# Attention stage: the transposes of a batch's probabilities all one period later, queries and keys last in a period

## The chip, the cores and the metric

The kernel runs on one core of one Trainium2 chip. The metric is the device time of one execution in microseconds. TensorE (PE in the rows, PEld its weight loads), VectorE (DVE), ScalarE (ACT), GpSimd (POOL) and SyncE (SP, which issues DMAs) each run their own queue in order and wait for one another by semaphores.

## The reference

The program is one transformer-like block on 64 images with text tokens: a tokenizer (patches, local and global attention) gives 5 tokens of 256 channels per image, 77 text tokens are joined to them, so T = 82 tokens per batch entry and 64 entries; then attention with a relative bias, then a mixture of 8 low-rank experts. The change is in the attention:

```python
qkv = (xn @ w_qkv + b_qkv).reshape(b, t, 3, H, hd)        # b 64, t 82, H 16 heads of hd 16
q, k, v = (qkv[0], qkv[1], qkv[2])
scores = jnp.einsum('bhqd,bhkd->bhqk', q, k) * scale
attn = jax.nn.softmax(scores + bias, axis=-1)             # bias: a function of query - key, per head
out = jnp.einsum('bhqk,bhkd->bhqd', attn, v)
out = jnp.transpose(out, (0, 2, 1, 3)).reshape(b, t, dim)
return out @ w_out + b_out
```

xn is a layer norm of a layer norm of the tokens; the result is added to the tokens. All in f32.

## The kernel before

Three blocks follow one another, with a barrier between: tokenizer (to about 205 us), attention (to about 667 us), experts. `attention_block` holds the 64 x 82 = 5248 tokens as 41 tiles of 128 and works in periods, one per batch entry b, with three more to drain (`for b in range(NB + 3)`). The order within a period is written out by hand, separately for each engine; an engine does its work in that order and waits where a semaphore isn't there yet.

The pieces of TensorE's work, all in f32, are:
- `xT(n)` transposes a normalised token tile n (one tile in 41 of the periods); ScalarE copies it to `hT` (`copy_xT`). GpSimd normalises the tile (`prepare`) and VectorE makes its statistics (`normal_stats`).
- `qk(q, j)` makes the queries (j = 0, 1) or keys (j = 2, 3) of half of the heads, for four batch entries at once (a quad q, 328 tokens): four products a quad, one per period, in the quad before. VectorE reads each with two instructions that scale it and add bias terms (`read_qk`, L981) into `qT` or `kT`, which hold two quads.
- `val(b)` makes the values of one entry; ScalarE copies them to `vv` (`copy_val`).
- `scores(b)` makes the 16 score matrices of 82 x 82 in four banks `psS` (32 small matmuls, L825). It waits for the last read of its quad's queries and keys, and for the reads of the scores of b - 1.
- VectorE's `shift(b, half)` takes the largest score of each row and subtracts it, in two halves, into `prob`; ScalarE's `exponent(b, half)` takes the exponential in place.
- `turn(b, g)`, g = 0 to 3, transposes four of the 16 matrices into `psP` (L834), which is one bank; ScalarE copies it to `probT` (`copy_probT`, L934), and the next turn waits for that copy.
- `weigh(b)` multiplies `probT` by the values (L847) and by ones (L852), which gives outputs and denominators, each denominator repeated over the 32 channels of its head pair. VectorE's `normalise` takes the reciprocal (L1005) and multiplies.
- `project(n)` is the output projection of a token tile (in 41 of the periods, three behind); ScalarE copies it and GpSimd adds it to the tokens.

`xT`, `qk`, `val` and `project` share two banks `psQ` in turn: `uses` lists them in TensorE's order, a use takes bank `place % 2` and waits in `free` until the use before the last has been read, by ScalarE or, for `qk`, by VectorE. `turned(b)` and `projected(b)` give the tiles of a period.

TensorE's order in period b: scores(b), weigh(b - 2), turn(b - 1, 2), xT, qk, turn(b - 1, 3), val(b + 1), turn(b, 0), project, turn(b, 1). The last two turns of an entry are so made one period after its first two. There is no qk from period 60 on. ScalarE's order matches: copy turn 2, copy tile, exponent 0, copy turn 3, exponent 1, copy values, copy turn 0, copy projection, copy turn 1. VectorE's: shift 0, shift 1, read qk, normalise(b - 2), statistics.

Of the kernel before, what the change touches and what calls it, by code (L numbers as in the profile page):

```python
# [13 lines left out]
NB, CIN, IMG = 64, 3, 96  # L14
# [622 lines left out]
def attention_block(nc, S, I, A, W, H, ident_all, out):  # L637

    NTL = NB * T // 128
    NQ = NB // 4  # L640
# [6 lines left out]
    def turned(b):  # L647
        return [n for n in range(NTL) if turn_at[n] == b]

    def projected(b):  # L650
        return [n for n in range(NTL) if last_of[n] == b - 3]
# [7 lines left out]
    uses = [("xT", 0), ("xT", 1), ("xT", 2)] + [("qk", j) for j in range(4)] + [("val", 0), ("xT", 3), ("xT", 4), ("xT", 5)]  # L659
    for b in range(NB + 3):  # L660
        uses += [("xT", n) for n in turned(b)]
        if b // 4 + 1 < NQ:
            uses.append(("qk", 4 * (b // 4 + 1) + b % 4))
        if b + 1 < NB:
            uses.append(("val", b + 1))
        uses += [("project", n) for n in projected(b)]
    place = {use: k for k, use in enumerate(uses)}
    by_act = {use: 1 + sum(u[0] != "qk" for u in uses[:k]) for k, use in enumerate(uses) if use[0] != "qk"}
    by_dve = {use: 1 + sum(u[0] == "qk" for u in uses[:k]) for k, use in enumerate(uses) if use[0] == "qk"}

    with ExitStack() as ctx:
# [30 lines left out]
        def bank(use):  # L702
            return psQ[:, place[use] % 2, :]
# [67 lines left out]
        def _(te):  # L771
# [16 lines left out]
            def xT(n):  # L788

                te.wait_ge(S["xh_ready"], n + 1)  # L790
                free(("xT", n))
                for c in range(2):
                    mm = te.transpose(bank(("xT", n))[:, 128 * c:128 * c + 128], xh[:, n % 3, 128 * c:128 * c + 128], ident_all[:])
                mm.then_inc(S["xT_done"], 1)
# [11 lines left out]
            def val(b):  # L806

                te.wait_ge(S["psQ_act"], by_act["xT", tiles_of[b // 4]])
                free(("val", b))
                a = T * b % RH  # L810
                for c in range(2):
                    mm = te.matmul(bank(("val", b))[0:T, 0:C], hT[:, c, a:a + T], wv[:, c, :], start=(c == 0), stop=(c == 1))  # L812
                mm.then_inc(S["val_done"], 1)
# [15 lines left out]
            def turn(b, g):  # L829

                te.wait_ge(S["prob_ready"], 2 * b + g // 2 + 1)
                te.wait_ge(S["probT_ready"], 4 * b + g)
                for s in range(4):
                    mm = te.transpose(psP[0:T, s * T:s * T + T], prob[:, b % 2, g, s, :], ident_all[0:T, 0:T])  # L834
                mm.then_inc(S["turn_done"], 1)
# [20 lines left out]
            def project(n):  # L856

                te.wait_ge(S["att_ready"], last_of[n] + 1)
                free(("project", n))
                a = 128 * n % RA  # L860
                for c in range(2):
                    mm = te.matmul(bank(("project", n))[:, 0:C], attT[:, c, a:a + 128], wout[:, c, :], start=(c == 0), stop=(c == 1))  # L862
                mm.then_inc(S["project_done"], 1)
# [8 lines left out]
            for b in range(NB + 3):  # L872
                if b < NB:
                    scores(b)
                if 0 <= b - 2 < NB:
                    weigh(b - 2)
                if 0 <= b - 1 < NB:
                    turn(b - 1, 2)
                for n in turned(b):
                    xT(n)  # L880
                if b // 4 + 1 < NQ:
                    qk(b // 4 + 1, b % 4)
                if 0 <= b - 1 < NB:
                    turn(b - 1, 3)
                if b + 1 < NB:
                    val(b + 1)
                if b < NB:
                    turn(b, 0)
                for n in projected(b):
                    project(n)  # L890
                if b < NB:
                    turn(b, 1)

        @block.scalar
        def _(act):
            def copy_xT(n):

                act.wait_ge(S["xT_done"], n + 1)
                done = (128 * n + 128 - RH + T - 1) // T
                if done > 0:  # L900
                    act.wait_ge(S["val_done"], done)
                for a, lo, size in pieces(128 * n, 128, RH):
                    ins = act.activation(hT[:, :, a:a + size],  # L903
                                         bank(("xT", n))[:, 0:256].rearrange("p (c t) -> p c t", c=2)[:, :, lo:lo + size], ACT.Copy)
                ins.then_inc(S["psQ_act"], 1)

            def copy_val(b):

                act.wait_ge(S["val_done"], b + 1)
                if b >= 4:  # L910
                    act.wait_ge(S["weigh_done"], b - 3)
                v4 = bank(("val", b))[0:T, 0:C].rearrange("p (s a d) -> p s a d", s=8, a=2)
                pair = vv[:, b % 4, :, :, :].rearrange("p s a (h d) -> p s (a h) d", h=2)[:, :, 0:4:3, :]
                act.activation(pair, v4, ACT.Copy).then_inc(S["psQ_act"], 1)

            def copy_project(n):

                act.wait_ge(S["project_done"], n + 1)
                if n >= 2:
                    act.wait_ge(S["res_ready"], n - 1)  # L920
                act.activation(po[:, n % 2, :], bank(("project", n))[:, 0:C], ACT.Copy).then_inc(S["psQ_act"], 1)  # L921

            def exponent(b, half):

                act.wait_ge(S["shifted"], 2 * b + half + 1)
                act.activation(prob[:, b % 2, 2 * half:2 * half + 2, :, :], prob[:, b % 2, 2 * half:2 * half + 2, :, :],  # L926
                               ACT.Exp).then_inc(S["prob_ready"], 1)

            def copy_probT(b, g):

                act.wait_ge(S["turn_done"], 4 * b + g + 1)
                if g == 0 and b >= 2:
                    act.wait_ge(S["weigh_done"], b - 1)
                act.activation(probT[:, b % 2, g, :, :].rearrange("p s t -> p (s t)"), psP[0:T, 0:4 * T],  # L934
                               ACT.Copy).then_inc(S["probT_ready"], 1)

            for n in range(3):
                copy_xT(n)
            act.wait_ge(S["vv_clear"], 1)
            copy_val(0)  # L940
            for n in range(3, 6):
                copy_xT(n)
            for b in range(NB + 3):
                if 0 <= b - 1 < NB:
                    copy_probT(b - 1, 2)
                for n in turned(b):
                    copy_xT(n)
                if b < NB:
                    exponent(b, 0)
                if 0 <= b - 1 < NB:  # L950
                    copy_probT(b - 1, 3)
                if b < NB:
                    exponent(b, 1)
                if b + 1 < NB:
                    copy_val(b + 1)
                if b < NB:
                    copy_probT(b, 0)
                for n in projected(b):
                    copy_project(n)
                if b < NB:  # L960
                    copy_probT(b, 1)

        @block.vector
        def _(v):
# [9 lines left out]
            def read_qk(q, j):  # L974

                v.wait_ge(S["qk_done"], 4 * q + j + 1)
                if q >= 2:
                    v.wait_ge(S["scores_done"], 4 * (q - 1))
                dst, scal, add, t = (qT, ownq, qadd, j) if j < 2 else (kT, own, kadd, j - 2)
                for a in range(2):  # L980
                    ins = v.scalar_tensor_tensor(out=dst[:, q % 2, a, t, :].rearrange("p (b t) -> p b t", b=4),  # L981
                                                 in0=bank(("qk", 4 * q + j))[:, 0:QT].rearrange("p (b t) -> p b t", b=4),
                                                 scalar=scal[:, a:a + 1], in1=add[:, a, t, :].unsqueeze(1).to_broadcast([128, 4, T]),
                                                 op0=ALU.mult, op1=ALU.add)
                ins.then_inc(S["psQ_dve"], 1)
# [55 lines left out]
            for b in range(NB + 3):  # L1041
                if b < NB:
                    shift(b, 0)
                    shift(b, 1)
                if b // 4 + 1 < NQ:
                    read_qk(b // 4 + 1, b % 4)
                if 0 <= b - 2 < NB:
                    normalise(b - 2)
                for n in turned(b + 2):
                    if n not in early:  # L1050
                        normal_stats(n)


def expert_block(nc, S, I, R, W, H, ident_all, out):
# [439 lines left out]
```

## Time and profile before

| | us |
|---|---|
| median of 3 runs | 861.71 |
| lowest, highest | 855.84, 864.61 |
| the profiled execution | 861.1 |
| its span, first to last instruction | 859.3 |

The page of a profile gives each engine's busy time first, then the span in slices. The order of time lists instructions by their start; neighbours of one line are merged (x32 is 32 instructions), their time runs from the first's start to the last's end, and what stands in brackets is how long the engine was idle before them and what ended that. Matmuls overlap their neighbours by some tenths of a microsecond, so what a piece of work costs TensorE is read from start to start. Windows give busy time by stretch, with the granted TensorE clock, 1.00 being full speed.

### The profile page before, as it was taken

What the parts mean: (1) busy time and instruction counts of PE and PEld (TensorE: products, weight loads), DVE (VectorE), ACT (ScalarE), POOL (GpSimd) and SP (SyncE); (2) the same over time, 40 slices, a digit from 0 to 9 for tenths busy, and PEclk for the clock granted to TensorE, in tenths of its full rate; (3) what the DMA queues carried; (4) which work ended last, traced back from release to release, by engine and by line L of the source; (5) the groups of instructions that cost most, each with busy time, mean ns of one, the idle gap of its engine ahead of it and who ended that gap; (6) DMA issues with size and microseconds to landing.
All of it is one profiled execution on the core that took longest, in us unless ns stands there. A gap on an engine that the chain in (4) does not pass through costs nothing. (4 is left out here: it accounts for less than half of the span.)

```text
span 859.3 us, 24631 instructions
## 1 busy us (share of the span) xinstructions
PE 690.2 (80%) x10030; PEld 527.5 (61%) x10030; DVE 599.7 (70%) x1199; ACT 349.9 (41%) x793; POOL 285.6 (33%) x361
## 2 busy tenths in 40 slices
PE   1769696461479999999999999999988479999960
PEld 1657543320257777777777777777766368888850
DVE  0627657843459899999899998998885246766525
ACT  1211111000035555555555555555454335555533
POOL 2474200002272333333233333332000455667333
PEclk9879899675779999999999999999998769999995
DMA  8990100005910000000000000000000412222117
GB/s 158 225 311 8 37 1 0 1 12 178 306 23 8 15 16 14 15 16 21 14 9 21 15 15 16 15 15 15 21 14 15 98 56 74 71 81 76 51 65 272
DMA packets 34786, 51.42 MB, mean 60 GB/s; under 512 B 9044, under 2 KB 26292, under 8 KB 34548
## 3 DMA queue, kind: packets, MB, share of 16 engines
q1 hardware_dynamic: 29524, 39.57, 16.2%
q0 software_dynamic: 5152, 10.29, 4.2%
q8 instruction: 81, 1.33, 0.6%
q14 instruction: 29, 0.24, 0.1%
HBM read 36.91 MB, written 18.00 MB: 64 GB/s over the span
## 5 line engine op out<-in xcount | busy, mean ns | idle before, releaser
L934 ACT ACTIVATE probT<-psP 82x328 f32<-82x328 f32 x256 | 112.1, 438 | 161.4 <-PE psP L834 161.4
L993 DVE TENSOR_REDUCE mx<-psS 82x8 f32<-82x656 f32 x128 | 106.5, 832 | 42.4 <-PE psS L825 42.2
L834 PE MATMUL psP<-ident_all,prob 82*82 82x82 f32 x1024 | 117.3, 236 | 22.5 <-ACT probT L934 22.4
L834 PEld LDWEIGHTS psP<-ident_all,prob 82*82 82x82 f32 x1024 | 89.8, 120 | 65.6 <-issue 25.9
L755 POOL TENSOR_TENSOR h_flat<-h_flat,po 128x256 f32<-128x256 f32 x41 | 29.7, 725 | 263.7 <-ACT po L921 263.7
L995 DVE TENSOR_TENSOR prob<-psS,mx 82x656 f32<-82x656 f32 x128 | 107.1, 837 | 4.4
L926 ACT ACTIVATE prob<-prob 82x656 f32<-82x656 f32 x128 | 94.8, 741 | 3.1 <-DVE prob L995 3.1
L802 PE MATMUL psQ<-hT,early 128*128 128x328 f32 x256 | 83.1, 449 | 0.6 <-ACT hT L903 0.5
L1005 DVE RECIPROCAL rden<-psO 128x164 f32<-128x164 f32 x64 | 74.8, 1169 | 4.4 <-PE psO L852 4.4
L812 PE MATMUL psQ<-early,hT 128*82 128x256 f32 x256 | 66.7, 383 | 0.1
L825 PE MATMUL psS<-kT,qT 32*82 32x82 f32 x2048 | 53.6, 242 | 0.0
L802 PEld LDWEIGHTS psQ<-hT,early 128*128 128x128 f32 x256 | 44.2, 192 | 13.1 <-issue 1.3
L742 POOL TENSOR_SCALAR xh<-h_flat,a_mv,a_rst 128x256 f32<-128x256 f32 x41 | 50.2, 1224 | 4.5
L847 PE MATMUL psO<-probT,vv 82*32 82x82 f32 x2048 | 50.7, 239 | 0.5 <-ACT probT L934 0.5
L1269 ACT ACTIVATE f_hT<-psH 128x1024 f32<-128x1024 f32 x39 | 39.9, 1024 | 26.4 <-PE psH L1198 26.4
L862 PE MATMUL psQ<-wout,attT 128*128 128x256 f32 x164 | 46.7, 410 | 4.1 <-DVE kT L981 1.9
L1131 POOL DMA_INDIRECT entry_rows<-yv,slot_entry x39 | 39.9, 1023 | 30.2 <-ACT yv L1276 24.1
L852 PE MATMUL psO<-probT,one 82*32 82x82 f32 x2048 | 49.0, 236 | 0.0
L825 PEld LDWEIGHTS psS<-kT,qT 32*82 32x82 f32 x2048 | 43.8, 149 | 7.4 <-issue 0.3
L1210 PE MATMUL psT<-f_hT,w2as 128*64 128x128 f32 x624 | 44.5, 286 | 3.6 <-DVE t L1351 3.6
L1198 PE MATMUL psH<-t1T,w1bs 64*128 64x128 f32 x624 | 46.8, 291 | 0.0
L227 PE MATMUL tk_ps<-early 128*128 128x256 f32 (+1 forms) x180 | 45.9, 407 | 0.0
(218 smaller groups left out, 1216.5 us busy)
## 6 DMA issues: line engine op xcount, KB each, us to landing
img<-in_x SPq DMA_DIRECT2D x6, 1008.0 KB, 19.5
out<-h_flat SPq DMA_DIRECT2D x41, 128.0 KB, 2.5
fused_rows<-in_txt SPq DMA_DIRECT2D x1, 4928.0 KB, 25.1
h_flat<-entry_rows SPq DMA_DIRECT2D x6, 512.0 KB, 6.5
h_flat<-fused_rows SPq DMA_DIRECT2D x1, 2176.0 KB, 16.2
ex_w2a<-in_ff_w_A SPq DMA_DIRECT2D x1, 2048.0 KB, 11.2
ex_w1b<-in_ff_w_B SPq DMA_DIRECT2D x2, 1024.0 KB, 16.7
out<-h_flat SPq DMA_DIRECT2D x8, 256.0 KB, 4.8
```

Source lines behind the costliest of these rows:

```text
L742: pool.tensor_scalar(xh[:, n % 3, :], H[:, n, :], mv[:, n % 4, 0:1], rst[:, n % 4:n % 4 + 1], ALU.subtract, ALU.mult).then_inc(S["xh_ready ...
L802: mm = te.matmul(bank(("qk", 4 * q + j))[:, 0:QT], wqkv[:, c, 128 * j:128 * j + 128], hT[:, c, a:a + QT], start=(c == 0), stop=(c == 1))
L812: mm = te.matmul(bank(("val", b))[0:T, 0:C], hT[:, c, a:a + T], wv[:, c, :], start=(c == 0), stop=(c == 1))
L825: mm = te.matmul(psS[0:T, g, s:s + T], qT[rows, par, a, t, cols], kT[rows, par, a, t, cols], start=True, stop=True)
L834: mm = te.transpose(psP[0:T, s * T:s * T + T], prob[:, b % 2, g, s, :], ident_all[0:T, 0:T])
L847: te.matmul(psO[32 * g:32 * g + 32, t * T:t * T + T], vv[:, b % 4, 4 * t + g, a, :], probT[:, b % 2, g, 2 * t + a, :], start=(a == 0), sto ...
L852: mm = te.matmul(psO[32 * g:32 * g + 32, (2 + t) * T:(3 + t) * T], one2[:, a, :], probT[:, b % 2, g, 2 * t + a, :], start=(a == 0), stop=( ...
L926: act.activation(prob[:, b % 2, 2 * half:2 * half + 2, :, :], prob[:, b % 2, 2 * half:2 * half + 2, :, :], ACT.Exp).then_inc(S["prob_ready ...
L934: act.activation(probT[:, b % 2, g, :, :].rearrange("p s t -> p (s t)"), psP[0:T, 0:4 * T], ACT.Copy).then_inc(S["probT_ready"], 1)
L993: v.tensor_reduce(mx[:, half, :, :], s4, X, ALU.max).then_inc(S["max_ready"], 1)
L995: v.tensor_tensor(prob[:, b % 2, 2 * half:2 * half + 2, :, :], s4, mx[:, half, :, :].unsqueeze(3).to_broadcast([T, 2, 4, T]), ALU.subtract ...
L1005: v.reciprocal(rden[:], o3[:, 1, :, :]).then_inc(S["rden_ready"], 1)
```

## The change

In TensorE's order all four turns of entry b - 1 are made in period b, in the order scores(b), weigh(b - 2), turn 0, xT, val(b + 1), turn 1, project, turn 2, qk, turn 3. `uses` is rearranged so that qk is the last use of a period. ScalarE's order becomes copy turn 0, copy tile, copy values, copy turn 1, exponent 0, copy projection, copy turn 2, exponent 1, copy turn 3. VectorE reads qk last in a period, behind `normalise` and the statistics. No instruction is added or taken away; how denominators are made (spread over channels by `one2`) stays. The diff:

```diff
--- before.py
+++ after.py
@@ -659,11 +659,11 @@
     uses = [("xT", 0), ("xT", 1), ("xT", 2)] + [("qk", j) for j in range(4)] + [("val", 0), ("xT", 3), ("xT", 4), ("xT", 5)]
     for b in range(NB + 3):
         uses += [("xT", n) for n in turned(b)]
-        if b // 4 + 1 < NQ:
-            uses.append(("qk", 4 * (b // 4 + 1) + b % 4))
         if b + 1 < NB:
             uses.append(("val", b + 1))
         uses += [("project", n) for n in projected(b)]
+        if b // 4 + 1 < NQ:
+            uses.append(("qk", 4 * (b // 4 + 1) + b % 4))
     place = {use: k for k, use in enumerate(uses)}
     by_act = {use: 1 + sum(u[0] != "qk" for u in uses[:k]) for k, use in enumerate(uses) if use[0] != "qk"}
     by_dve = {use: 1 + sum(u[0] == "qk" for u in uses[:k]) for k, use in enumerate(uses) if use[0] == "qk"}
@@ -875,21 +875,21 @@
                 if 0 <= b - 2 < NB:
                     weigh(b - 2)
                 if 0 <= b - 1 < NB:
-                    turn(b - 1, 2)
+                    turn(b - 1, 0)
                 for n in turned(b):
                     xT(n)
+                if b + 1 < NB:
+                    val(b + 1)
+                if 0 <= b - 1 < NB:
+                    turn(b - 1, 1)
+                for n in projected(b):
+                    project(n)
+                if 0 <= b - 1 < NB:
+                    turn(b - 1, 2)
                 if b // 4 + 1 < NQ:
                     qk(b // 4 + 1, b % 4)
                 if 0 <= b - 1 < NB:
                     turn(b - 1, 3)
-                if b + 1 < NB:
-                    val(b + 1)
-                if b < NB:
-                    turn(b, 0)
-                for n in projected(b):
-                    project(n)
-                if b < NB:
-                    turn(b, 1)
 
         @block.scalar
         def _(act):
@@ -942,23 +942,23 @@
                 copy_xT(n)
             for b in range(NB + 3):
                 if 0 <= b - 1 < NB:
-                    copy_probT(b - 1, 2)
+                    copy_probT(b - 1, 0)
                 for n in turned(b):
                     copy_xT(n)
+                if b + 1 < NB:
+                    copy_val(b + 1)
+                if 0 <= b - 1 < NB:
+                    copy_probT(b - 1, 1)
                 if b < NB:
                     exponent(b, 0)
+                for n in projected(b):
+                    copy_project(n)
+                if 0 <= b - 1 < NB:
+                    copy_probT(b - 1, 2)
+                if b < NB:
+                    exponent(b, 1)
                 if 0 <= b - 1 < NB:
                     copy_probT(b - 1, 3)
-                if b < NB:
-                    exponent(b, 1)
-                if b + 1 < NB:
-                    copy_val(b + 1)
-                if b < NB:
-                    copy_probT(b, 0)
-                for n in projected(b):
-                    copy_project(n)
-                if b < NB:
-                    copy_probT(b, 1)
 
         @block.vector
         def _(v):
@@ -1042,13 +1042,13 @@
                 if b < NB:
                     shift(b, 0)
                     shift(b, 1)
-                if b // 4 + 1 < NQ:
-                    read_qk(b // 4 + 1, b % 4)
                 if 0 <= b - 2 < NB:
                     normalise(b - 2)
                 for n in turned(b + 2):
                     if n not in early:
                         normal_stats(n)
+                if b // 4 + 1 < NQ:
+                    read_qk(b // 4 + 1, b % 4)
 
 
 def expert_block(nc, S, I, R, W, H, ident_all, out):
```

## Rows read from the trace of the kernel before

**Rows 1.** The page, part 1: busy us, share of the span, instructions.
```profile
PE 690.2 (80%) x10030; PEld 527.5 (61%) x10030; DVE 599.7 (70%) x1199; ACT 349.9 (41%) x793; POOL 285.6 (33%) x361
```

**Rows 2.** Windows: stretch, length, busy us (instructions) by engine, granted clock, DMA.
```profile
300.00:600.00 300.00, 285.58 (x5696) 226.28 (x5695) 272.80 (x432) 163.35 (x384) 96.65 (x141) 1.00 0.05 16
...
659.00:662.00 3.00, 2.04 (x52) 1.89 (x56) 1.03 (x3) 0.72 (x2) 0.00 (x0) 0.70 0.10 32
```

**Rows 3.** Order of time, period 25: start, us, engine, line, operation, idle before.
```profile
404.59 0.83 PE L825 MATMUL psS<-kT,qT 32*82 32x82 f32 x32
...
405.35 0.78 PE L847 MATMUL psO<-probT,vv 82*32 82x82 f32 x32
...
405.49 0.84 DVE L993 TENSOR_REDUCE mx<-psS 82x8 f32<-82x656 f32 x1 [0.36 <-PE psS L825]
...
406.63 0.48 PE L834 MATMUL psP<-ident_all,prob 82*82 82x82 f32 x4
...
406.95 0.38 PE L793 MATMUL psQ<-ident_all,xh 128*128 128x128 f32 x2
...
407.18 1.27 PE L802 MATMUL psQ<-hT,early 128*128 128x328 f32 x4
...
408.28 0.45 PE L834 MATMUL psP<-ident_all,prob 82*82 82x82 f32 x4
...
408.56 1.03 PE L812 MATMUL psQ<-early,hT 128*82 128x256 f32 x4
...
408.73 1.01 DVE L981 SCALAR_TENSOR_TENSOR qT<-psQ,ownq,qadd 128x328 f32<-128x328 f32 x2
...
409.11 0.74 ACT L926 ACTIVATE prob<-prob 82x656 f32<-82x656 f32 x1
...
409.43 0.45 PE L834 MATMUL psP<-ident_all,prob 82*82 82x82 f32 x4
...
410.01 0.44 ACT L934 ACTIVATE probT<-psP 82x328 f32<-82x328 f32 x1
...
410.59 0.46 PE L834 MATMUL psP<-ident_all,prob 82*82 82x82 f32 x4 [0.71 <-ACT probT L934]
...
410.98 0.83 PE L825 MATMUL psS<-kT,qT 32*82 32x82 f32 x32
```

**Rows 4.** Order of time, period 27, which has a projection and no tile.
```profile
417.60 0.83 PE L825 MATMUL psS<-kT,qT 32*82 32x82 f32 x32
...
419.96 1.31 PE L802 MATMUL psQ<-hT,early 128*128 128x328 f32 x4
...
421.11 0.45 PE L834 MATMUL psP<-ident_all,prob 82*82 82x82 f32 x4
...
421.74 1.01 DVE L981 SCALAR_TENSOR_TENSOR kT<-psQ,own,kadd 128x328 f32<-128x328 f32 x2
...
422.26 0.45 PE L834 MATMUL psP<-ident_all,prob 82*82 82x82 f32 x4
...
422.90 1.10 PE L862 MATMUL psQ<-wout,attT 128*128 128x256 f32 x4 [0.19 <-DVE kT L981]
...
423.84 0.45 PE L834 MATMUL psP<-ident_all,prob 82*82 82x82 f32 x4
...
424.22 0.83 PE L825 MATMUL psS<-kT,qT 32*82 32x82 f32 x32
```

**Rows 5.** Order of time at the stage's start and in its last periods.
```profile
248.60 1.22 POOL L742 TENSOR_SCALAR xh<-h_flat,a_mv,a_rst 128x256 f32<-128x256 f32 x1
...
654.32 0.45 PE L834 MATMUL psP<-ident_all,prob 82*82 82x82 f32 x4 [0.62 <-ACT probT L934]
...
654.81 0.44 ACT L934 ACTIVATE probT<-psP 82x328 f32<-82x328 f32 x1
...
660.41 1.32 PE L847 MATMUL psO<-probT,vv 82*32 82x82 f32 x32 [0.53 <-ACT probT L934]
```

## The prediction

> **What bounds the kernel now.** I read the page first, then the engines' busy time by windows, then the order of time through single periods of the attention stage. The page gives TensorE 80% of the span, the most of any engine [rows 1]. The change touches the attention stage alone, which holds 64 periods between 241 and 660 us, so the windows matter more: between 300 and 600 us TensorE is busy 285.58 of 300 us at a granted clock of 1.00 (full speed, 2.4 GHz), VectorE 272.80 and ScalarE 163.35 [rows 2]. TensorE's order sets the pace, and VectorE has some 9% to spare. The order of time through one period shows how. I count from the start of `scores`: for a period with a token tile and no projection [rows 3] the starts are scores 0, weigh 0.76, turn 2.04, token tile 2.36, qk 2.59, turn 3.69, val 3.97, turn 4.84, turn 6.00, and the next scores 6.39. So what follows what costs, start to start: scores 0.76, weigh 1.28, turn 0.32 before a token tile, token tile 0.23, qk 1.10 (1.15 where it follows a turn directly [rows 4]), turn 0.28 before val, val 0.87, turn 0.38 before scores, projection 0.94 [rows 4]. The exception is a turn that follows a turn with nothing between: 4.84 to 6.00, of which the row puts 0.71 down to the wait for ScalarE's copy, since `psP` is one bank and the copy must empty it. With a projection between the two turns that wait goes, but the projection starts 0.64 after its turn, 0.19 of it waiting for VectorE's read of the qk bank [rows 4].
>
> By `turned` and `projected`, periods 2 to 59 are 17 with a token tile only (6.39 us each), 16 with tile and projection (410.98 to 417.60: 6.62), 20 with a projection only (417.60 to 424.22: 6.62) and 5 with neither (6.39 less the tile: 6.2) [rows 3, 4].
>
> **The new order on TensorE, steady periods.** Nothing is added or removed: the same matmuls, copies and reads, no DMA moved. The order becomes scores, weigh, T0, tile, val, T1, projection, T2, qk, T3. All four turns work on exponentials of the period before, so none waits for an exponential any more; T0 to T1 is covered by val, T2 to T3 by qk, T1 to T2 by the projection only, where there is one.
>
> A bare turn pair costs 1.10: where ScalarE is free the copy starts 0.49 after the turn, and the next turn starts 0.58 after that copy does [rows 3, 5], 1.07; 1.16 was seen behind another copy; I take 1.10. Then:
> - Projection only: T0 2.04, val 2.36, T1 3.23, projection 3.55, T2 4.49, qk 4.81, T3 5.96, scores 6.34. Before 6.62: 0.28 less, times 20 is 5.6.
> - Tile and projection: the tile adds 0.23, so 6.57: 0.05 less, times 16 is 0.8.
> - Tile only: T1 3.46, T2 4.56 (bare pair), qk 4.88, T3 6.03, scores 6.41: 0.03 more, times 17 is 0.5.
> - Neither: T1 3.23, T2 4.33, scores 6.18: 0.02 less, times 5 is 0.1.
> Sum: 6.0 us less. The gain is small, since the wait for the copy moves from the last pair of turns to T1 and T2 and stays 0.7 long in 22 periods; what goes is the projection's wait for the qk bank. Bounds: with 1.07 to 1.16 for the bare pair the 22 periods give -0.7 to +1.3, and every start being read to 0.01 or 0.02 gives another 1, so 4 to 8 less.
>
> Does ScalarE keep up? In its new order (copy T0, copy tile, copy val, copy T1, exponential 0, copy projection, copy T2, exponential 1, copy T3) the longest chain is: val ends about 3.6, its copy to 4.0, copy T1 about 3.97 to 4.4, exponential 0 from 4.3 (its input is there since about 2.6, half-way through the shifts, which end by 4.14 [rows 3]), copy T2 at 5.05 to 5.25, exponential 1 about 5.4 to 6.2, copy T3 at T3 + 0.49. Each copy is there when TensorE wants it. The tightest is new: weigh of the next period needs copy T3, ready 1.07 to 1.10 after T3 starts, and weigh comes 0.38 + 0.76 = 1.14 after T3. That is a tie with 0.04 to spare. I cost it at nothing; if the cover is short by 0.05 it costs 3 us over 58 periods.
>
> **The wait that is added.** The queries and keys of the next four batches are made one product per period, the fourth in periods 3, 7, ... 59. `scores` of the period after reads them at once: it waits for `by_dve["qk", 4*(b//4)+3]`. Before, that read began at 4.14 and ended at 5.15 [rows 3], long before scores at 6.4. Now qk starts last but one, at 4.8 to 5.05; its matmuls take 1.31 [rows 4]; a VectorE instruction starts about 0.07 after the last matmul it waits for (scores 0 + 0.83, reduction 0.90 [rows 3]); the two reads last 1.01; and TensorE goes on 0.15 after the end of such a read (421.74 + 1.01 to 422.90 [rows 4]). That is 2.54 from the start of qk to scores, against 1.15 + 0.38 = 1.53 by TensorE's own order. So 1.01 us of pause in each of 15 periods: 15.2 us more. VectorE is free to read at once: its 272.80 us over some 46 periods [rows 2] are 5.93 a period, 1.01 of it these reads; the other 4.9, begun at 0.90, end near 5.9, before qk's matmuls do (6.1 to 6.4). Behind the waiting scores stand weigh and all four turns of the period, and VectorE and ScalarE, which live on them; nothing catches up, because the other periods are TensorE's own order. In the other periods the read hides: it ends where the scores are just done (qk + 2.4 against 1.53 + 0.90 = 2.43). Bounds: 0.85 if the matmuls' modelled end is late by 0.15, 1.2 if statistics come in the way: 13 to 18 us.
>
> **Ends of the stage.** At the start the two turns of period 0 leave it, and scores of period 1 no longer wait for exponentials. But the token tile of period 1 comes from GpSimd, whose normalisation runs 248.60 to 249.82 whatever TensorE does [rows 5], and it now stands ahead of val and all but one turn. So of 2.5 us by TensorE's order I keep 0.9 less (bounds 0 to 2.5). At the end period 64 has four turns, bare, where it had two: 2 x 1.10 = 2.2 more, and 0.7 for the weigh ahead of them, whose last turn was bare too. Against it stand 0.65 less over periods 60 to 63 (0.16, 0.33 and 0.16, the fourth is in the 0.7). The last weigh already ran at 0.70 of the clock, 1.32 instead of 0.78 us for one half [rows 2, 3, 5]; with two more turns at low load I add 0.5. Sum of the end: 2.75 more (2 to 4).
>
> **On the clock.** In [rows 2] it stayed at 1.00 through 300 us with a pause of 0.71 in most of the periods without a projection, and was down in the last 3 us of the stage, where two bare turns and a wait stood in a row. The Trainium skill ("TensorE: Matmul & The Clock Gate", part 4, PE-mode transpose) says that transposes don't count as a busy engine for the clock; by that, four of them in a row are worse than two, and the trace agrees in kind with its 0.70. The 0.5 us above comes from the rows alone; by the rule it would be nearer to 1.5.
>
> **Sum.** -6.0 + 15.2 - 0.9 + 2.75 = +11.0 us. The profiled execution took 861.1 us, the median of the runs shown is 861.71, so the two can be taken as one: 861.7 + 11.0 = 872.7, which I give as 872.5.
>
> **The rivals.**
> - A. The mechanism as summed, 872.5. For it: the wait is in the code, all its parts have rows. Own range 866 to 879. Chance 0.72.
> - B (the other side). The pause before scores is hidden: the fourth qk read ends in time and costs nothing. Then -6.0 - 0.9 + 2.75 = -4.2, 857.5, faster than before though within 1%. It decides the sign where the pause is under 0.28 us. It would need the read to start before qk's matmuls end. Against it: qk is last but one and one turn of 0.38 is all its cover. Chance 0.07.
> - C. Weigh waits for the copy of T3 in every period, because the exponential 1 ahead of that copy on ScalarE is late. The exponential lasts 0.74 [rows 3] and has about 0.4 to spare; were it used up and the copy 0.25 late, 58 x 0.25 = 14.5 more: 887. For it: the tie of 0.04. Chance 0.12.
> - D. The turns gain more than I see: the bare pair T1 and T2 costs no more than a covered one (22 x 0.75 = 16.5 less than summed): 856. Against it: `psP` stays one bank and the bare pair has a row at 0.62 of wait even where ScalarE is idle [rows 5]. Chance 0.04.
> - E. The 1 us pauses drop the clock. One half of weigh takes 1.32 instead of 0.78 at the lower level (1.2 GHz) [rows 3, 5], a factor of 1.7; a period of 6.4 would become about 10.8, and 15 of them add 66: 938. The Trainium skill ("TensorE: Matmul & The Clock Gate", HAM oscillation) ties a fall to gaps longer than these. Against it: pauses of 0.71 left the clock at 1.00 [rows 2, 3]. Chance 0.03. 0.02 remain for what I have not thought of.
>
> **How the numbers follow.** The likeliest is A, 872.5. The range 865 to 881 takes A's bounds (13 - 8 - 2.5 + 2 = +4.5 to 18 - 4 + 0 + 4 = +18, rarely all at one end) and the mild part of C; it leaves out B, D, E and the rest of C, about 2 in 10. About 1% (8.6 us: under 853.1, over 870.3) is what a measurement of this kernel can tell from no change. Slower by over 1%: seven in ten of A, 0.50, and C, E, 0.14: 0.64. Faster by over 1%: half of D and a little of B, 0.03. Within: 0.33.
>
> **What would show it.** Right: scores starts in the periods after 3, 7, ... wait about 1.0 us for VectorE's `kT` read (L981), some 15 us in the table of waits; projection's wait for `qT`/`kT` gone; TensorE's wait for the copies of `probT` stays near 18 us; periods with projection only 6.3 us, tile only 6.4; TensorE busy share between 300 and 600 us falls a little. Wrong: scores not waiting at all (B), `psO` matmuls waiting for `probT` (C), turns of 0.3 us spacing in periods without projection (D), a granted clock under 1.00 between 300 and 600 us (E).

## The result, and the profile after

| | before | after |
|---|---|---|
| median, us | 859.22 (9 runs) | 866.81 (9 runs) |
| lowest, highest | 855.84, 864.61 | 863.58, 868.17 |
| the profiled execution | 861.1 | 866.31 |
| its span | 859.3 | 864.5 |

The ratio is 1.008, with a 95% interval of 1.0055 to 1.0105: the change costs 0.8%, some 7 us. The prediction was 872.5 us (865 to 881), so slower it is, by less than forecast: within 1%, to which it gave a chance of 0.33, and not over 1%, to which it gave 0.64.

The wait that the prediction put at every fourth period is there. This is who waited for whom in the kernel after between 240 and 640 us (engine and line, what it waited for: us in total, times, longest):

```profile
PEld psS L825 <- DVE kT L981: 15.4, 15, 1.1
PE psP L834 <- ACT probT L934: 14.3, 23, 0.6
PE psS L825 <- DVE kT L981: 12.7, 15, 0.9
```

`scores` waits 15 times for the `kT` read, 12.7 us together (0.83 to 0.91 each); the wait of a turn for its copy is still there (23 times, up to 0.6, where [rows 3] had 0.71); the projection's wait for the qk bank [rows 4] is in no line any more. The same in order of time, in the kernel after, from the last turns of period 3 (which ends a quad) through period 4 (projection, no tile) to the next scores:

```profile
265.47 0.45 PE L834 MATMUL psP<-ident_all,prob 82*82 82x82 f32 x4 [0.62 <-ACT probT L934]
265.76 1.31 PE L802 MATMUL psQ<-hT,early 128*128 128x328 f32 x4
...
266.90 0.45 PE L834 MATMUL psP<-ident_all,prob 82*82 82x82 f32 x4
...
267.10 1.02 DVE L981 SCALAR_TENSOR_TENSOR kT<-psQ,own,kadd 128x328 f32<-128x328 f32 x2
...
268.18 0.83 PE L825 MATMUL psS<-kT,qT 32*82 32x82 f32 x32 [0.83 <-DVE kT L981]
...
269.08 0.83 DVE L993 TENSOR_REDUCE mx<-psS 82x8 f32<-82x656 f32 x1 [0.95 <-PE psS L825]
...
271.42 0.45 PE L834 MATMUL psP<-ident_all,prob 82*82 82x82 f32 x4
...
271.70 1.07 PE L862 MATMUL psQ<-wout,attT 128*128 128x256 f32 x4
...
272.61 0.45 PE L834 MATMUL psP<-ident_all,prob 82*82 82x82 f32 x4
...
272.89 1.31 PE L802 MATMUL psQ<-hT,early 128*128 128x328 f32 x4
...
274.04 0.45 PE L834 MATMUL psP<-ident_all,prob 82*82 82x82 f32 x4
...
274.42 0.83 PE L825 MATMUL psS<-kT,qT 32*82 32x82 f32 x32
```

qk starts at 265.76, its read at 267.10, 1.34 later; the read ends at 268.12 and scores starts at 268.18. VectorE then waits 0.95 itself for those scores. The next period has none of this: the projection follows its turn by 0.28 (0.64 in [rows 4]) and the whole period takes 6.24 us instead of 6.62. Over the steady stretch the two effects nearly cancel: 300 us hold 5692 matmuls, where they held 5696. The window of the kernel after (columns as in [rows 2]):

```profile
300.00:600.00 300.00, 280.77 (x5692) 225.60 (x5691) 274.38 (x431) 164.46 (x383) 96.66 (x141) 1.00 0.05 16
```

Read from start to start of scores, the periods 2 to 59 of both kernels, mean us of each kind:

| kind | before | after | after, where the next quad begins |
|---|---|---|---|
| projection only (20) | 6.62 | 6.23 | 7.18 (5 of them) |
| tile and projection (16) | 6.62 | 6.45 | 7.35 (4) |
| tile only (17) | 6.39 | 6.33 | 7.24 (5) |
| neither (5) | 6.2 | 6.1 to 6.25 | 7.01 (1) |

And the attention stage in four parts, from traces of one execution each (starts of scores of periods 0, 2, 60, 63, and of the last projections):

| kernel | 0 to 2 | 2 to 60 | 60 to 63 | 63 to the last projections | sum |
|---|---|---|---|---|---|
| before | 13.58 | 377.97 | 18.41 | 11.58 | 421.54 |
| after | 15.46 | 379.91 | 19.22 | 14.58 | 429.17 |

The stage is 7.6 us longer, as much as the medians differ (7.6). The two spans differ by 5.2 only, because the profiled execution of the kernel after began its attention work 1.7 us sooner (its first matmul at 221.24 instead of 222.98, after DMAs that the change doesn't touch).

### The profile page after: what moved, and what is told of

It reads as the page before. It is cut to its first block and busy times, and to the rows that moved or that the text cites. A ratio compares the mean times of both kernels' runs of the same rounds, so it can differ in the third digit from the quotient of the medians.

```text
span 864.5 us, 24631 instructions
## 1 busy us (share of the span) xinstructions
PE 689.2 (80%) x10030; PEld 530.6 (61%) x10030; DVE 603.6 (70%) x1199; ACT 352.1 (41%) x793; POOL 286.4 (33%) x361
## 5 line engine op out<-in xcount | busy, mean ns | idle before, releaser
L802 PE MATMUL psQ<-hT,early 128*128 128x328 f32 x256 | 85.4, 458 | 0.6 <-ACT hT L903 0.5
L825 PE MATMUL psS<-kT,qT 32*82 32x82 f32 x2048 | 53.8, 242 | 12.7 <-DVE kT L981 12.7
```

The costliest lines, as they stand in the source:

```text
L802: mm = te.matmul(bank(("qk", 4 * q + j))[:, 0:QT], wqkv[:, c, 128 * j:128 * j + 128], hT[:, c, a:a + QT], start=(c == 0), stop=(c == 1))
L825: mm = te.matmul(psS[0:T, g, s:s + T], qT[rows, par, a, t, cols], kT[rows, par, a, t, cols], start=True, stop=True)
```

## The experiments

Theory Q is that of the prediction: the cost is scores waiting for the fourth qk read, and the gain is the projection no longer waiting for the qk bank; both come from qk standing last, none from the turns. Its rival R: the gain comes from the turns, which no longer depend on exponentials of their own period. Each ratio is to runs of the kernel before in the same series. In one series the kernel before took 907.0 us, some 45 us longer, outside the attention stage: with the tile first, it has there 377.86 us between scores 2 and 60 and 421.39 in the four parts together (421.54 in the table). The four kernels of that series (the fourth product alone last, the tile first in the kernel before, the last turns, the three together) are read by their ratio and by the parts of the stage only.

**One part alone: the turns.**

```diff
-                    turn(b - 1, 2)
+                    turn(b - 1, 0)
...
-                    turn(b - 1, 3)
+                    turn(b - 1, 1)
...
-                if b < NB:
-                    turn(b, 0)
+                if 0 <= b - 1 < NB:
+                    turn(b - 1, 2)
                 for n in projected(b):
                     project(n)
-                if b < NB:
-                    turn(b, 1)
+                if 0 <= b - 1 < NB:
+                    turn(b - 1, 3)
```

This is against the kernel before, whose `uses` and VectorE order it keeps; ScalarE's copies of the turns follow.

> One part alone: all four turns in the period after, but qk and its read where the kernel before has them (behind the token tile; VectorE reads ahead of normalise); order scores, weigh, turn 0, tile, qk, turn 1, val, turn 2, projection, turn 3. Theory Q (the cost is scores waiting for the fourth qk read, the gain is the projection no longer waiting for the qk bank): both are gone here, since the projection again follows qk by one use and scores waits for nothing. Periods with a projection 6.6 us, with a tile only 6.3, no wait of scores, and the costs of the stage's ends (3 to 5 us) stay: 0 to +4 us against before. Rival R (what gains is that turns no longer depend on the exponentials of their own period): periods with a projection fall to 6.2 to 6.45 here too, and the time is 5 to 10 us under before.

Measured 864.8 us, ratio 1.003 (1.0005 to 1.0055). Between scores 2 and 60 it takes 377.94 us, the kernel before 377.97; periods with a projection are 6.62, with a tile only 6.39. Who waited, between 300 and 600 us:

```profile
PE psP L834 <- ACT probT L934: 12.1, 17, 0.7
PE psQ L862 <- DVE kT L981: 1.4, 7, 0.2
```

The projection waits for the qk bank as before and scores waits for nothing. The last part is 15.19 us instead of 11.58. So the turns a period later bring nothing in the steady periods and cost some 3 us at the end: rival R falls.

**The other part alone: qk last.**

```diff
-                    turn(b - 1, 0)
+                    turn(b - 1, 2)
...
-                    turn(b - 1, 1)
+                    turn(b - 1, 3)
...
-                if 0 <= b - 1 < NB:
-                    turn(b - 1, 2)
+                if b < NB:
+                    turn(b, 0)
                 if b // 4 + 1 < NQ:
                     qk(b // 4 + 1, b % 4)
-                if 0 <= b - 1 < NB:
-                    turn(b - 1, 3)
+                if b < NB:
+                    turn(b, 1)
```

This is against the changed kernel, whose `uses` and VectorE order it keeps; ScalarE's copies of the turns follow, and exponential 0 goes ahead of the copy of the values.

> The other part alone: turns 0 and 1 of an entry stay in its own period, qk and its read go to the end; ScalarE takes exponential 0 ahead of the copy of the values, so that turn 0 has it in time. Order scores, weigh, turn 2, tile, val, turn 3, projection, turn 0, qk, turn 1. Theory Q: 15 waits of scores of 0.9 us as in the changed kernel, periods 6.2 to 6.45 otherwise, as the changed kernel; the tail is as before, so 3 to 4 us under the changed kernel: +2 to +5 against before. Rival R: without the turns a period later the steady periods stay at 6.4 to 6.6, and with the 15 waits the time is +12 to +16 against before.

Measured 869.34 us, ratio 1.0102 (1.0062 to 1.0142), some 8 us over before: more than the 2 to 5 that Q gave, less than the 12 to 16 of R. The waits between 240 and 640 us:

```profile
PEld psS L825 <- DVE kT L981: 15.4, 15, 1.1
PE psS L825 <- DVE kT L981: 12.7, 15, 0.9
```

The 15 waits are those of the changed kernel to the tenth, and a period with a projection only is 6.23 again, though the turns stand where they stood before. The last part is 11.62, as before. Two things make it slower than expected: periods with a tile are 6.48 instead of 6.33 and 6.45 (383.28 us between scores 2 and 60, 3.4 more than the changed kernel), since my order for ScalarE puts an exponential ahead of the values' copy; and the granted clock of this execution fell to 0.50 in period 62 (9.07 us instead of 6.13). The steady part speaks for Q: the gain of 0.39 in projection-only periods and the 12.7 us of wait both belong to qk alone.

**The wait alone, in the kernel before.**

```diff
-                if b // 4 + 1 < NQ:
+                if b // 4 + 1 < NQ and b % 4 < 3:
                     qk(b // 4 + 1, b % 4)
...
                 for n in projected(b):
                     project(n)
+                if b // 4 + 1 < NQ and b % 4 == 3:
+                    qk(b // 4 + 1, b % 4)
                 if b < NB:
                     turn(b, 1)
```

> The kernel before with the wait alone: in periods 3, 7, ... 59 the fourth qk product goes between the projection and turn 1, and its read to the end of VectorE's period; the other 49 periods and the turns stay as they were. Theory Q: scores waits 0.8 to 0.9 us of TensorE's own time 15 times for the kT read; those periods are 0.6 to 0.9 us longer (the projection's wait for the qk bank goes in the nine that have one), +9 to +13 against before. Rival (the pause is made up in the next periods): under +4.

Ratio 1.0165 (1.0118 to 1.0212), 14 us. Of the waits, the part between 300 and 600 us:

```profile
PE psP L836 <- ACT probT L938: 13.8, 23, 0.7
PE psS L827 <- DVE kT L985: 9.2, 11, 0.8
```

The stage is 393.98 us long between scores 2 and 60, 16.0 more than before: the 43 other periods are unchanged to 0.01 us and the 15 are 0.73 (tile only) to 1.34 us longer (7.12, 7.88, 7.96). Nothing is made up in the next period; that rival falls. It is more than I expected, because with qk gone from between turns 2 and 3 the second of them waits for the copy in these 15 periods, 0.62 us where nothing is left between the two and 0.40 where a tile is. So the edit adds more than the wait under test: between scores 2 and 60, `scores` waits 12.6 us for the read, and the turns wait 18.6 us in place of 15.6.

**The wait taken away from the changed kernel.** Each product one period earlier:

```diff
-                if b // 4 + 1 < NQ:
-                    qk(b // 4 + 1, b % 4)
+                if b + 5 < 4 * NQ:
+                    qk((b + 5) // 4, (b + 5) % 4)
```

`uses` and `read_qk` follow, and qk(1, 0) and its read stand ahead of period 0.

> The changed kernel with the one suspected wait taken away: each qk product is made one period earlier (product b + 5 instead of b + 4; the first of quad 1 ahead of period 0), so that the fourth of a quad is read a whole period before its scores. Same work. Theory Q: the 15 waits (12.7 us on TensorE in its row, 13.8 by period lengths) go, nothing else changes but 0 to 2 us at the start: 12 to 14 us under the changed kernel, some 6 under before. Rival: if the wait only moved work that VectorE must do anyway, the loop is then held by VectorE (busy 5.9 of 6.2 us a period) and under 6 us are gained.

Measured 853.07 us, ratio 0.9911 (0.9877 to 0.9944): against the changed kernel's 1.008 that is 1.7%, 14 us. Between scores 2 and 60 it takes 365.68 us, 14.2 less than the changed kernel, and the ends of quads are now as long as the other periods (6.23, 6.33, 6.45). 0.3 of the 14.2 is period 59 (5.93 us), which has no product any more. The price of the wait is read from this stretch; the medians hold more than the wait, since in the traces the start is 2.4 us shorter too, period 62 is 1.6 shorter at full clock and the end is 0.6 longer. The window and what is left of the waits:

```profile
300.00:600.00 300.00, 289.44 (x5893) 232.93 (x5895) 283.63 (x444) 170.66 (x396) 98.10 (x143) 1.00 0.05 16
```

```profile
PE psP L834 <- ACT probT L935: 10.6, 17, 0.6
```

VectorE goes from 274.38 to 283.63 of 300 us and still doesn't hold the loop, so that rival falls as well. Taking the wait away gives back 14 us, and adding it costs 12.6 us in its own row, inside a total of 14 to 16 us that holds other waits too: this step is settled.

**The start.** The stage's first two periods were 1.9 us longer after the change, where 0.9 less was forecast. TensorE in period 1 of the kernel after, and two windows:

```profile
247.90 0.44 PE L793 MATMUL psQ<-ident_all,xh 128*128 128x128 f32 x2 [1.54 <-POOL xh L742]
248.17 1.87 PE L812 MATMUL psQ<-early,hT 128*82 128x256 f32 x4
...
251.75 2.47 PE L802 MATMUL psQ<-hT,early 128*128 128x328 f32 x4
...
254.69 0.96 PE L825 MATMUL psS<-kT,qT 32*82 32x82 f32 x32
```

```profile
248.00:251.00 3.00, 2.59 (x10) 1.56 (x10) 1.96 (x4) 1.20 (x5) 1.47 (x3) 0.53 0.00 0
251.00:254.00 3.00, 2.79 (x8) 1.85 (x9) 0.00 (x0) 1.78 (x4) 1.95 (x2) 0.50 0.00 0
```

It waits 1.54 us for the tile from GpSimd and then the clock is at its lower level (0.50, 1.2 GHz) for six microseconds, val takes 1.87 and qk 2.47. Theory H: the wait for the tile made the clock fall. The test lets GpSimd prepare that tile first:

```diff
+            for n in turned(1):
+                prepare(n)
             for n in early:
                 add_row(n)
...
-                        prepare(n)
+                        if b > 0:
+                            prepare(n)
                         add_row(n)
```

> The changed kernel with one thing at the start: GpSimd normalises the token tile of period 1 before the seven additions of the bias row (4.8 us) instead of behind them. Theory H (the start lost 3 us against the prediction because TensorE waited 1.5 us for that tile and the granted clock then fell to 0.50 until 254 us): no wait of the tile, clock 1.00 from period 1 on, scores 0 to scores 2 about 12.5 instead of 15.5 us: 3 us under the changed kernel. Rival: the clock falls anyway, since the first periods are thin; then 0 to 1.5 us are gained.

```profile
248.49 0.39 PE L796 MATMUL psQ<-ident_all,xh 128*128 128x128 f32 x2
248.71 1.04 PE L815 MATMUL psQ<-early,hT 128*82 128x256 f32 x4
...
250.95 1.31 PE L805 MATMUL psQ<-hT,early 128*128 128x328 f32 x4
...
252.47 0.83 PE L828 MATMUL psS<-kT,qT 32*82 32x82 f32 x32
```

No wait, val 1.04, qk 1.31, and scores 0 to 2 take 11.15 instead of 15.46 us: 4.3 less, more than the 3 expected. The median is 861.63 us, ratio 1.001 (0.9987 to 1.0033), 0.7% under the changed kernel's; in the traces 1.6 us more are period 62, which was at the lower clock in the changed kernel's and isn't here. The control is the same edit in the kernel before:

> Control to the run with the tile first: the kernel before with the same change of GpSimd's order at the start. There TensorE waited 0.16 us for the tile of period 1 and its clock was at 1.00 by then. If the 3 to 5 us gained in the changed kernel came from the wait that the changed order made: 0 to 0.5 us gained here, within 1 us of before. Rival (the additions of the bias row slow VectorE or ScalarE in both kernels): 3 us gained here too.

Ratio 0.9991 (0.9964 to 1.0018), scores 0 to 2 in 13.54 instead of 13.58 us: nothing. So it is the changed order, which asks for the tile sooner, that ran into GpSimd; the turns alone a period later do it too (the tile waited for 1.51 us). That the wait of 1.5 us brings the clock down each time isn't shown. With the turns alone later it came down too (qk 2.29 us, scores 0 to 2 in 14.34). Of two kernels below with the changed kernel's order in period 1, the one with the denominators moved waited 1.48 us and took 15.33 us from scores 0 to 2 at the lower clock (qk 2.47); the one with the last turns moved waited 1.43 us and took 12.68, at full clock in period 1 (val to the next turn 0.86). So the clock fell behind three of the four such waits, and in no kernel whose wait there was under 1 us.

**The end.** The turns 0 and 1 of the last entry alone back in period 63, behind its turn 3 (period 64 leaves them out, and ScalarE's copies follow):

```diff
                 if 0 <= b - 1 < NB:
                     turn(b - 1, 3)
+                if b == NB - 1:
+                    turn(b, 0)
+                    turn(b, 1)
```

> The changed kernel with turns 0 and 1 of the last entry alone back in their own period (63), behind its turn 3, so that period 64 has two turns as before. If the longer end of the stage (3 us in period 63 and after) comes from the two bare turns that moved into period 64: the two turns are bare in period 63 just as well and stand ahead of the weigh that waits for the copy of turn 3, whose wait they now cover: 0.7 to 1.2 us less from scores 63 to the last projection, the other 2 us stay. Rival (it is the lower clock of thin periods): no gain, the distance from scores 63 to the last projection stays at 14.6 us, give or take 1.

No gain, where 0.7 to 1.2 us were expected: 14.56 us from scores 63 to the last projections, 14.58 in the changed kernel; ratio 1.0067 (1.0034 to 1.01). The total is the rival's number, but the parts are not. The wait of the first weigh is covered (weigh starts 0.38 us behind its turn instead of 0.98), and the 0.6 us so gained are lost behind it at the lower clock, where the second half of that weigh takes 1.02 us instead of 0.75 and the next two turns start 1.39 us apart instead of 1.10. This is how the stage ends in the kernel after:

```profile
663.72 0.45 PE L834 MATMUL psP<-ident_all,prob 82*82 82x82 f32 x4 [0.62 <-ACT probT L934]
664.79 0.74 PE L834 MATMUL psP<-ident_all,prob 82*82 82x82 f32 x4 [0.62 <-ACT probT L934]
666.06 1.32 PE L847 MATMUL psO<-probT,vv 82*32 82x82 f32 x32 [0.53 <-ACT probT L934]
```

A turn takes 0.45 us and 0.74 a microsecond later. The end holds eight turns from scores 63 on where the kernel before has six, and takes 3.0 us more: 2.1 for the two bare turns, 0.6 for the wait of the first weigh and 0.3 for the lower clock behind the last turn. In all traces it took 14.56 to 15.40 us with eight turns and 10.97 to 11.62 with six. That it makes no difference where the two stand isn't shown, since the clock differed.

**The three together**, qk one period ahead, GpSimd's tile first and the last turns moved (the diffs above):

> The changed kernel with all three: qk one period ahead, GpSimd's tile of period 1 first, turns 0 and 1 of the last entry in period 63. If the three costs are separate, 853.1 of the first alone less 0.5 to 1 for the end; the start was already without a pause there (tile wait gone since qk stood ahead of it), so nothing for the tile: 852, ratio to before 0.990.

Ratio 0.9929 (0.9901 to 0.9957), no better than the wait taken away alone (0.9911). The edits aren't separate: scores 0 started 23.2 us after the stage's first matmul, 18.0 in the changed kernel and 21.0 with qk one period ahead alone. That this comes from qk(1, 0) ahead of period 0 together with a tile more to prepare is likely, but no run parts the two.

**A version that beats both.** What remains of TensorE's waits is the bare pair. In the periods without a projection, the denominators' half of weigh (its second loop, now a function of its own) can stand between turns 1 and 2:

```diff
+            def denominators(b):
...
                 if 0 <= b - 2 < NB:
                     weigh(b - 2)
+                    if projected(b) or b >= NB:
+                        denominators(b - 2)
...
                     turn(b - 1, 1)
+                if 0 <= b - 2 < NB and not (projected(b) or b >= NB):
+                    denominators(b - 2)
```

> The changed kernel with the bare pair covered: in the 22 periods without a projection the second half of weigh (the denominators, 0.69 us) stands between turns 1 and 2, where TensorE waits 0.62 us for ScalarE's copy. If the bare pair costs what its row says, these periods fall from 6.33 to 5.65 by TensorE's order; VectorE (5.9 us of work a period) then holds some of it back: 6.33 to 5.9, 22 x 0.4 = 9 us under the changed kernel, at most 15. Rival (VectorE already sets the steady pace through the scores bank): under 3 us gained.

> qk one period ahead as in the run before it, but the first product of quad 1 inside period 0 instead of ahead of it (two products in period 0). Same steady periods as that run; the start of the stage 1 to 3 us shorter: ratio to before 0.988 (that run: 0.991).

> Both together: qk one period ahead and the bare pair covered by the denominators. TensorE's order asks for 5.65 us in periods without a projection and 6.23 to 6.45 in the others; VectorE asks for about 6.0 on average: a mean of 6.1 to 6.2 over 58 periods against 6.33 now, 8 to 12 us under the run before it: ratio to before 0.975 to 0.98. Rival: VectorE holds the loop at 6.3, then no gain.

The first, in the changed kernel: 854.78 us, ratio 0.9951 (0.9923 to 0.9979); periods with a tile only 5.81 instead of 6.33, with neither 5.59 instead of 6.12, 10.6 us less between scores 2 and 60. The expectations of the other two mean by "the run before it" the one with qk one period ahead, and for the third the second. The second has the first product of quad 1 inside period 0 (`products(0)` is [4, 5], then b + 5): 851.55 us, 0.9911 (0.9887 to 0.9934), the steady part 365.78 us, as there; the start was 2.7 us longer in scores 0 to 2 and 2.8 shorter ahead of it, so nothing came of moving it. The third, both: 837.96 us, ratio 0.9752 (0.9733 to 0.9771), 354.22 us between scores 2 and 60, 11.6 less than the second. The medians are 13.6 apart, over the 8 to 12 expected; in the traces period 62 is another 1.6 us shorter, at full clock. Its window:

```profile
300.00:600.00 300.00, 300.00 (x6072) 240.18 (x6065) 290.31 (x455) 175.60 (x406) 97.31 (x142) 1.00 0.05 17
```

TensorE waits for nothing in 300 us, and VectorE is at 290 of 300: in this stretch the order is at the end of what covering TensorE's waits can give. It is 2.5% under the kernel before and 3.3% under the changed one.

## Why the prediction was right, and where its sizes were off

**The wait.** Right in place and count, 15.2 us forecast. It is 13.8 by the lengths of periods (about 0.90 to 0.95 each), 13.9 by the run that takes it away, without its period 59. The step mis-sized is the handing on: 2.54 from the start of qk to scores, measured 2.42. TensorE went on 0.06 after the end of the read, not 0.15; the 0.15 of [rows 4] was not such a hand-over alone.

**The gain in the steady periods.** Forecast 6.0 us less, bounds 4 to 8; measured 11.9 (20 x 0.39, 16 x 0.17, 17 x 0.06, 5 x 0.08). The mechanism was right: the projection's wait goes and the bare pair stays at 0.62. The size came out beyond the bounds. It failed on hundredths: I took 0.32 for the step from a turn to what follows it, which [rows 3] show only for the turn behind weigh; behind the other turns it is 0.28 (there too, 408.28 to 408.56). The projection is 0.91 and not 0.94, the bare pair 1.07 and not 1.10. That makes 0.06 to 0.12 a period, and 58 periods make 5.9 us of it. My bound of 1 us for reading errors leaves room for 0.02 a period at most, and a step read from the wrong place stood several times in each.

**The start.** Forecast 0.9 less, measured 1.9 more. I saw that the tile came at 249.82 [rows 5] and took that only as a limit on the gain. The step that failed is that I gave this wait no price beyond the time it lasts: in the traced execution the clock was low for 6 us behind it. Where it stayed up behind the same wait (the last turns moved), scores 0 to 2 took 12.68 us, 0.9 less than before, as forecast; so nearly all of the 2.8 us is the clock's. Why it falls in one execution and not in another stays open. With the tile early the start is 2.4 us shorter than before, the 2.5 of TensorE's order that the prediction named.

**The end.** Forecast 2.75 more, measured 3.8: 3.0 from scores 63 on (forecast 3.4: 2.2, 0.7 and 0.5 for what measured 2.1, 0.6 and 0.3) and 0.8 over periods 60 to 63 (forecast 0.65 less). The latter is one period at the lower clock, 7.53 us in this trace; in the run with the tile first, with the same order, it took 5.92 and the three periods 0.8 less than before, as forecast.

**The sum.** 15.2 - 6.0 - 0.9 + 2.75 = 11.0 was forecast; 13.8 - 11.9 + 1.9 + 3.8 = 7.6 was measured. The errors are -1.4 for the wait, -5.9 for the gain, +2.8 for the start and +1.0 for the end; they partly cancel. That the time fell into the range is so in part luck: the two terms of the steady part were 7.3 us off, and half of that was hidden by the two ends, where the clock was low in the traced execution. With the start at 12.68 us and period 62 at 5.92, both seen with the same order, the four parts would add up to 3.2 us more than before, less than the +4.5 at the lower end of the prediction's bounds.

**The rivals.** B (the wait hidden) is refuted by its 15 rows. C didn't come: copy T3 of the period above started at 267.39, in time, and no weigh waits in the steady stretch. D (the bare pair costs nothing) is refuted by 23 waits, and its prize of 16.5 us was too high: with the denominators between the two turns 10.6 to 11.6 us were gained. E (the 1 us pauses drop the clock) is refuted: 1.00 from 300 to 600 us with 11 pauses in it. The rule of the Trainium skill ("TensorE: Matmul & The Clock Gate", part 4, PE-mode transpose), that transposes don't count as a busy engine in the same way, fits the falls behind runs of bare turns at the end; but in the same places other executions kept full clock, so the trace can't tell it from a load that is thin in any other way.

## What to carry to other kernels

When a producer is moved to the end of a period, look for the period in which its consumer is first in line: an average hides it, since 3 of 4 products have time and the fourth stalls everything. Moving the product one whole period earlier keeps the cover and loses the stall. A step that recurs in every period must be read from its own place in the order (what follows what), because a few hundredths of a microsecond times the periods outweigh the mechanism that one is arguing about.

## What was not expected of the hardware

TensorE's granted clock at the thin ends of the stage differs from one execution to the next with the same order of work: period 62, with the changed kernel's order, took 5.92 or 5.93 us in five kernels, 7.53 in the changed kernel itself and in one more, and 9.13 in another; with qk last only, it was 9.07. The windows of the changed kernel there:

```profile
643.00:646.00 3.00, 1.76 (x15) 1.16 (x14) 2.93 (x5) 2.48 (x6) 0.00 (x0) 1.00 0.00 0
646.00:648.00 2.00, 2.00 (x77) 1.80 (x80) 1.01 (x2) 0.83 (x2) 0.00 (x0) 0.89 0.04 8
648.00:650.00 2.00, 2.00 (x38) 1.60 (x31) 1.93 (x4) 0.21 (x1) 0.00 (x0) 0.50 0.00 0
```

Three microseconds of bare turns (TensorE busy 1.76 of 3.00) stand ahead of the fall to 0.50. Such a fall is worth 1.6 to 3.2 us and makes single traces differ by as much as a step of the sum.
